# The depthwise convolution of a layer-0 attention: one fused operation per tap on VectorE, or a multiplication and an addition per tap on GpSimd

## What is computed

```python
q = x @ Wq + bq
k = (x @ Wk + bk) * scaling
v = x @ Wv + bv
lepe = lax.conv_general_dilated(v, dw_w, window_strides=(1, 1), padding=((2, 2), (2, 2)),
        dimension_numbers=('NHWC', 'HWIO', 'NHWC'), feature_group_count=C) + dw_b      # 5 x 5, per channel
attn = jnp.einsum('bhnd,bhmd->bhnm', qr, kr) + mask       # qr, kr: q and k rotated by sin and cos
out = jnp.einsum('bhnm,bhmd->bhnd', jax.nn.softmax(attn, axis=-1), vr)
out = out.transpose(0, 2, 1, 3).reshape(B, H, W, C)
out = out + lepe
return out @ Wo + bo
```

## Time and profile before

| | |
|---|---|
| runs, median | 3836.91 us |
| the profiled execution | 3838.61 us |
| its span, first to last instruction | 3836.5 us |
| TensorE (PE) busy, share of the span | 3551.4 us, 93% |
| VectorE (DVE) | 2785.7 us, 73% |
| ScalarE (ACT) | 2080.6 us, 54% |
| GpSimd (POOL) | 1448.0 us, 38% |
| the layer-0 attention | some 245 to 2706 us of the span |

### The profile page before, as it was taken

One profiled execution on the slowest core, in us unless ns is written; L12 is line 12 of the kernel. 1 busy time (PEld: TensorE's weight loads), 2 busy tenths in 40 slices (PEclk: granted clock), 3 DMA queues, 4 the chain that ended last, 5 costly groups with the idle time before them and its releaser, 6 DMA issues. The chain is left out here.

```text
span 3836.5 us, 97899 instructions
## 1 busy us (share of the span) xinstructions
PE 3551.4 (93%) x30782; PEld 2678.6 (70%) x30782; DVE 2785.7 (73%) x6801; ACT 2080.6 (54%) x3661; POOL 1448.0 (38%) x671
## 2 busy tenths in 40 slices
PE   7759999999999999999999999999399999999776
PEld 4437777777777777777777777777277777778555
DVE  6858777777777777877777777778465555644598
ACT  3336666666666666666666666666145454545433
POOL 2335555555555555555555555555100000000223
PEclk8879999999999999999999999999699999999788
DMA  5444224223224223322422422221520111000001
GB/s 168 140 116 105 80 90 123 89 84 106 88 87 126 88 67 101 110 86 95 110 74 95 118 89 88 70 87 60 158 79 14 40 54 40 1 1 0 28 13 38
DMA packets 122409, 307.36 MB, mean 80 GB/s; under 512 B 15609, under 2 KB 85292, under 8 KB 101548
## 3 DMA queue, kind: packets, MB, share of 16 engines
q1 hardware_dynamic: 122284, 305.78, 25.8%
HBM read 251.43 MB, written 54.31 MB: 80 GB/s over the span
## 5 line engine op out<-in xcount | busy, mean ns | idle before, releaser
L729 DVE CUSTOM_DVE_ANT_0 c_S<-c_Sps,mask_tiles 128x768 f32<-128x768 f32 x1728 | 1607.5, 955 | 531.8 <-PE c_Sps L781 521.1
L670 ACT ACTIVATE c_PT<-c_Tps 128x512 f32<-128x512 f32 x2592 | 1457.6, 602 | 927.4 <-PE c_Tps L792 861.4
L642 POOL TENSOR_SCALAR c_S<-c_S,c_row_max 128x2304 f32<-128x2304 f32 x576 | 1264.4, 2195 | 1195.6 <-DVE c_row_max L740 1195.6
L792 PE MATMUL c_Tps<-ident,c_S 128*128 128x128 f32 x10368 | 1457.8, 274 | 4.1 <-ACT c_PT L670 4.1
L792 PEld LDWEIGHTS c_Tps<-ident,c_S 128*128 128x128 f32 x10368 | 1219.7, 140 | 261.1 <-issue 119.1
L781 PE MATMUL c_Sps<-c_K,c_Q 96*128 (+1 forms) x3456 | 853.6, 328 | 59.2 <-DMA c_Q<-q_parts 40.9
L805 PE MATMUL c_Ops<-c_PT,c_V 128*32 128x256 f32 x10368 | 648.8, 383 | 0.8 <-ACT c_PT L670 0.8
L781 PEld LDWEIGHTS c_Sps<-c_K,c_Q 96*128 96x128 bf16 x3456 | 325.5, 98 | 209.5 <-issue 136.0
L805 PEld LDWEIGHTS c_Ops<-c_PT,c_V 128*32 128x32 f32 x10368 | 304.6, 109 | 222.4 <-ACT c_PT L670 46.4
L1242 DVE TENSOR_SCALAR_CACHE_REDUCE l_S<-l_Sps 128x384 f32<-128x384 f32 x432 | 240.5, 558 | 270.7 <-PE l_Sps L1089 242.7
L1019 ACT ACTIVATE l_PT<-l_Tps 128x384 f32<-128x384 f32 x432 | 196.5, 491 | 395.2 <-PE l_Tps L1110 395.2
(11 more groups left out here) (209 smaller groups left out, 1914.6 us busy)
## 6 DMA issues: line engine op xcount, KB each, us to landing
mask_tiles<-in_mask SPq DMA_DIRECT2D x144, 1152.0 KB, 7.7
numerators<-c_O SPq DMA_DIRECT2D x288, 64.0 KB
l_num<-numerators SPq DMA_DIRECT2D x8, 2304.0 KB, 8.5
q_parts<-f_parts SPq DMA_DIRECT2D x12, 576.0 KB, 3.4
k_parts<-f_parts SPq DMA_DIRECT2D x12, 576.0 KB
c_Q<-q_parts SPq DMA_DIRECT2D x72, 96.0 KB
c_K<-k_parts SPq DMA_DIRECT2D x8, 864.0 KB, 8.6
c_vpad<-v_padded SPq DMA_DIRECT2D x8, 756.0 KB, 15.0
```

The source lines that it names most:

```text
L642: pool.tensor_scalar(S[:, slot, :], S[:, slot, :], -1.0, row_max[:, slot:slot + 1], ALU.mult, ALU.add).then_inc(shifted, 1)
L670: act.activation(dst, src, ACT.Exp, scale=-1.0).then_inc(exp_done, 1)
L729: dve.tensor_tensor_reduce(out=S[:, r % ROW_SLOTS, cols(CH, c)].rearrange("p (k n) -> p k n", k=2), in0=Sps[:, n % S_SLOTS, :, 0:GW], in1= ...
L792: last = pe.transpose(Tps[:, g % T_SLOTS, cols(P, k)], S[:, (2 * b + t) % ROW_SLOTS, cols(P, kt)], ident[:, :])
```

## The change

The tap leaves VectorE. GpSimd now issues, between the shifts, a multiplication of the window with the tap's weight into one of two buffers `product` (for tap 0 straight into `conv`) and, one row later, an addition of `product` to `conv`. The multiplication stands behind the shifts of rows 0, 3 and 5 of a pair, the addition behind the shifts of rows 1, 4 and 6. The first multiplication of a head waits for the loaded half and for the store of the half two heads before. There are 25 taps instead of 27, so the last pair of a head has one; the zero fill of `conv` goes, and the padded image is 52 columns shorter. The rows of GpSimd, before in a loop of four, are written out over two heads (144 rows) in a loop of four turns. SyncE waits for 25 steps per head instead of 28.

```diff
-TAP_SLOTS = 27
-HALF_IN = (TAP_SLOTS - 1) // 5 * WP + 4 + HALF_OUT
+HALF_IN = (TAPS - 1) // 5 * WP + 4 + HALF_OUT
...
+        product = sb("product", [P, 2, N // 2])
...
-        TAP_ROWS = (2, 5, 7)
+        TAP_ROWS = (0, 3, 5)
...
-                sp.wait_ge(conv_step, CONV_STEPS * (h + 1))
+                sp.wait_ge(conv_step, TAPS * (h + 1))
...
+            def shift(ip, r):
+                slot = r % ROW_SLOTS
+                pool.wait_ge(max_ready, ROWS * ip + r + 1)
+                alone(pool)
+                pool.tensor_scalar(S[:, slot, :], S[:, slot, :], -1.0, row_max[:, slot:slot + 1],
+                                   ALU.mult, ALU.add).then_inc(shifted, 1)
+
+            def scale_tap(h, hp, tap):
+                window = vpad[:, hp * HALF_IN + tap // 5 * WP + tap % 5:][:, 0:HALF_OUT].rearrange("p (h w) -> p h w", w=WP)
+                image = (product[:, tap % 2, :] if tap else conv[:, hp, :]).rearrange("p (h w) -> p h w", w=W)
+                if tap == 0:
+                    pool.wait_ge(vpad_in, 16 * (h + 1))
+                    pool.wait_ge(conv_stored, 16 * (h + 1))
+                    alone(pool)
+                pool.tensor_scalar(image, window[:, :, 0:W], taps[:, tap:tap + 1], None, ALU.mult).then_inc(
+                    tap_scaled if tap else conv_step, 1)
+
+            def add_tap(h, hp, tap):
+                pool.wait_ge(tap_scaled, (TAPS - 1) * h + tap)
+                alone(pool)
+                pool.wait_ge(conv_step, TAPS * h + tap)
+                alone(pool)
+                pool.tensor_tensor(conv[:, hp, :], conv[:, hp, :], product[:, tap % 2, :], ALU.add).then_inc(conv_step, 1)
+
             with pool.Fori(0, HEADS // 2) as hh:
                 for hp in range(2):
-                    pool.wait_ge(conv_stored, 16 * (2 * hh + hp + 1))
-                    alone(pool)
-                    pool.memset(conv[:, hp, :], 0.0).then_inc(conv_step, 1)
-                    with pool.Fori(0, ROUNDS) as i:
-                        for slot in range(ROW_SLOTS):
-                            pool.wait_ge(max_ready, ROW_SLOTS * ((2 * hh + hp) * ROUNDS + i) + slot + 1)
-                            alone(pool)
-                            pool.tensor_scalar(S[:, slot, :], S[:, slot, :], -1.0, row_max[:, slot:slot + 1],
-                                               ALU.mult, ALU.add).then_inc(shifted, 1)
+                    h = 2 * hh + hp
+                    for qp in range(HEAD_PAIRS):
+                        for r in range(ROWS):
+                            shift(h * HEAD_PAIRS + qp, r)
+                            if r in TAP_ROWS:
+                                tap = len(TAP_ROWS) * qp + TAP_ROWS.index(r)
+                                if tap < TAPS:
+                                    scale_tap(h, hp, tap)
+                            if r - 1 in TAP_ROWS:
+                                tap = len(TAP_ROWS) * qp + TAP_ROWS.index(r - 1)
+                                if 0 < tap < TAPS:
+                                    add_tap(h, hp, tap)
...
-                dve.scalar_tensor_tensor(out=dst, in0=window[:, :, 0:W], scalar=taps[:, bass.ds(tap, 1)],
-                                         in1=dst, op0=ALU.mult, op1=ALU.add).then_inc(conv_step, 1)
...
-                    if r in TAP_ROWS:
-                        conv_tap(ip, TAP_ROWS.index(r))
```

More of the change, by code:

```diff
@@ L516, in layer0_core @@
         vpad_in, conv_step, conv_stored = sem("vpad_in"), sem("conv_step"), sem("conv_stored")
-        taps_padded = sem("taps_padded")
+        tap_scaled = sem("tap_scaled")
         HEAD_PAIRS = TILES // 2
@@ L523, in layer0_core @@
         ROWS = 2 * B
-        CONV_STEPS = TAP_SLOTS + 1
-        TAP_ROWS = (2, 5, 7)
+        TAP_ROWS = (0, 3, 5)
         COLS = 4
@@ L609, in _ @@
                 load_head(h + 1)
-                sp.wait_ge(conv_step, CONV_STEPS * h + 1)
+                sp.wait_ge(conv_step, TAPS * h + 1)
                 alone(sp)
@@ L629, in _ @@
             pool.memset(V[:, :, :], 1.0).then_inc(v_ones, 1)
-            pool.memset(taps[:, TAPS:TAP_SLOTS], 0.0).then_inc(taps_padded, 1)
-            ROUNDS = HEAD_PAIRS * ROWS // ROW_SLOTS
+            def shift(ip, r):
[4 more added lines that the diff above has]
+                                   ALU.mult, ALU.add).then_inc(shifted, 1)
@@ L754, in pair @@
                         chunk(ip, p, r, c)
-                    if r in TAP_ROWS:
-                        conv_tap(ip, TAP_ROWS.index(r))
-            dve.wait_ge(taps_padded, 1)
             pair(0, 0, start=True)
@@ L1783, in hybrid @@
         ident = ctx.enter_context(nc.sbuf_tensor("ident", [P, P], F32))
-        taps = ctx.enter_context(nc.sbuf_tensor("taps", [P, TAP_SLOTS], F32))
+        taps = ctx.enter_context(nc.sbuf_tensor("taps", [P, TAPS], F32))
         conv_bias = ctx.enter_context(nc.sbuf_tensor("conv_bias", [P, 1], F32))
```

## The result

The changed kernel takes 3882.46 us (median of 4 runs, 3879.5 to 3884.16), the kernel before 3836.11 beside it: ratio 1.0115, 95% interval 1.0103 to 1.0127, so 46 us slower. The forecast was no change, 3836.5 us, with 3812 to 3880; 3882 lies above the range. What happened is rival (a) in its effect, a multiplication dear enough to make GpSimd the bound. The reason given for it, the runs of the window (the 24 stretches of 48 contiguous elements that the shifted window consists of), is wrong.

What follows compares the result with a forecast made beforehand. TensorE, busy 495.40 of 500 us, was taken as the bound, with GpSimd's 31.4 us fitting a 34.04 us pair. Every term was 0 us, so 3836.5 us was predicted, range 3812 to 3880.

Steps and rivals of the forecast that it cites:

- rival (a): GpSimd multiplication: the window's runs cost more, from 45 ns a run GpSimd sets the beat; +98 us at 2.63 us; chance 0.10.
- the price of the multiplication: GpSimd, three multiplications a pair: 1.3 us each, from the shift's 1.10 us for 1152 elements plus 0.18 for 24 runs.
- The bound above: GpSimd multiplication, upper ends of its price: 2.63 us as the two-input form, far off 4.7 us by the selection's price.
- The runs' 7.4 ns: Window of the GpSimd multiplication: 7.4 ns a run from two selections of 284 and about 520 ns, 0.18 us for 24.
- The gaps: GpSimd, between instructions with a wait between them: 0.15 us for each of 14, 2.1 us a pair.
- the addition: GpSimd, three additions of 128x1152 a pair: 2.62 us each, priced from the same form in the last stage.
- the taps on VectorE as free: VectorE, 216 taps removed, some 4.45 us of a 34.04 us pair: TensorE was not waiting for them, 0 us.
- VectorE's waits for scores: VectorE in the attention stage: expected to rise by some 130 us in 1000, as time gained becomes waiting.
- rival (b): VectorE score additions blocked by GpSimd's two-input additions, 1.3 us each, three a pair: +280 us, 4120 us; chance 0.03.
- the replay of the shifts: GpSimd shifts replayed with the new work between: row 7, the tightest, 0.4 us later with 1.5 us left; 0 us.
- The light pair: Last pair of a head on GpSimd: only one tap, as 25 taps lie in 9 pairs.

Runs made afterwards that it cites:

- e1: Kernel of its own with only single GpSimd and VectorE operations, no attention: multiplication by a weight 3198 ns dense, 3197 ns in 24 runs.
- e4: The kernel before without the taps on VectorE, the convolution left out and its steps only counted: 3837.98 us, ratio 0.9999.
- e6: The changed kernel with the multiplication written as two operations, x times 1.0 times weight: 3837.89 us, ratio 0.9999 to the kernel before.
- e3: The changed kernel with the 25 taps of a head spread evenly over its 72 rows: 3838.69 us, ratio 1.0 to the kernel before.

## Why the prediction was wrong

- **The step that failed** is the price of the multiplication: "The shift has the same kind of instruction: 2195 ns for 2304 elements, so 1.10 us for 1152, the lower end", with 1.3 us taken. It measured 3.23. The shift has two operations and the multiplication one, and this difference, which the diff shows in its `None`, was not priced. The trace of before holds no GpSimd `tensor_scalar` with one operation. The likeness was taken from the name in the row.
- **The bound above** was drawn, at 2.63 us for the two-input form and 4.7 far off, and 3.2 lies between them. What failed next was the weight: rival (a) got 0.10, because its one reason, the runs, could be argued against. An operation that the trace doesn't hold needs a chance for being dear for a reason not thought of, above all where the sum says from which price it decides.
- **The runs' 7.4 ns** came from selections whose 32 "runs" are a pattern of their index; in memory their tile is dense. e1 shows 0 for runs in a multiplication. What the 236 ns between the two selections are for stays open; they differ in their comparison as well.
- **The gaps** of 0.15 us between instructions were too high. They were read from an instruction that waits for the one just before it; in e1, where each waits so, 0.1 us lies between two as well. In the change the waits are met a row earlier: the instructions follow each other at once, and the starts lie up to 0.04 us closer than the durations. 14 x 0.15 = 2.1 us a pair were not there, so the price from which GpSimd is the bound is (34.04 - 17.3 - 7.86) / 3 = 2.96 us, not 2.2. The excess at 3.21 is only 0.25 x 3, which is why the loss is 46 us and not over 200.
- **Right**: the addition (2.66 us for 2.62), the taps on VectorE as free (e4), VectorE's waits for scores up by 125 us in 1000 (some 130 predicted), the score additions unblocked (956 ns, so rival (b) didn't happen), and the conclusion of the replay of the shifts: with the multiplication at the cost that was assumed, no change results (e6). The 2.1 us of gaps in the sum were on the safe side there.
- **The light pair** was noted and not used. Its place matters: the same 25 taps spread over the head are free (e3). The prediction compared loads over a full pair, which is the right stretch for this placement, since 8 full pairs follow each other. The sum over a head as well (299.0 us, 33.2 a pair, under 34.04) would have shown that the same work fits even at 3.21 us a multiplication.

## What to carry to other kernels

Price an added instruction by a row that agrees in its number of operations and operands, not only in its name; where none exists, measure it alone or leave real weight on the side where it decides. An engine off the path hides work up to the load of the bounding engine over the stretch that the buffers bridge (how long that is was not measured here), so spread it evenly and write the sum for the fullest stretch. Before work is moved off an engine, look at what its removal alone would give: here 0, while moving one group of scores, which removed four stops of 0.28 us a pair, was worth 71 us.

## What the runs showed of the hardware

- GpSimd `tensor_scalar` on 128x1152 float32: with one operation 3.12 us (immediate) and 3.20 us (per-partition operand), with two 1.15 and 1.23 (1.30 with two per-partition operands). Multiplying by 1.0 first makes it 2.6 times faster. The Trainium skill, "GPSIMD Engine Reference", section "Engine selection", has operations with one input at roughly line rate; that fits the copy (1.15 us, where VectorE's took 1.22 in e1) and the form with two operations, not the one with one.
- Patterns of 24 or 48 runs cost GpSimd nothing more in a multiplication, an addition (2.62 us) or a copy, and VectorE nothing in its fused operation (1418 and 1419 ns).
- GpSimd worked at 97% of a stretch beside VectorE's score additions, which read PSUM and one SBUF tensor, without lengthening them (956 ns).
- GpSimd instructions whose waits are already met start 0 to 0.04 us before the recorded end of the one ahead of them (after, from 1195.69 us); where each waits for the one ahead, 0.1 us lies between them (e1).
